# Other PSUM banks for scores, query features and the output product, and other slots for their steps, in a fused graph-transformer kernel

## The reference

```python
# attention of layer i, per head (8 heads of 64, 256 random features)
qp = softmax_kernel(q, proj[i], True)        # exp(q @ proj.T - diag - max over features) + eps
o = einsum('bhmd,bhnm,bhn->bhnd', ctx, qp, d_inv)
x = x + o @ Wo[i] + bo[i]
y = layernorm(x, ln2_g[i], ln2_b[i])
x = x + gelu(y @ W1[i] + b1[i]) @ W2[i] + b2[i]      # 512 -> 2048 -> 512
# product-key memory on the normed sum of the branches
q1, q2 = halves of (x @ Wq + bq).reshape(-1, 8, 128)
s1t, i1 = top_k(q1 @ keys[:, 0].T, 8); s2t, i2 = top_k(q2 @ keys[:, 1].T, 8)   # 256 keys each
scores, best = top_k(all 64 sums of s1t and s2t, 8)  # -> 64 table rows per node
inner = einsum('bd,bhkd->bhk', x, w_down[indices])
out = einsum('bhk,bhkd->bd', relu(inner) * softmax(scores), w_up[indices])
```

## Time and profile before

| | us |
|---|---|
| median of 3 runs | 2603.11 (2601.43 to 2609.05) |
| the profiled execution, its own time | 2612.62 |
| its span in the trace | 2610.8 |
| PE busy / DVE / POOL / ACT over the span | 2223.4 (85%) / 1453.7 (56%) / 1034.6 (40%) / 742.2 (28%) |
| DMA, mean over the span | 204 GB/s |

### The profile page before, as it was taken

How to read it: one execution, slowest core, us unless ns; L and a number is a source line. 1 busy time by engine, 2 the same in 40 slices (tenths; PEclk the granted TensorE clock), 3 DMA queues, 4 the chain that set the end, 5 groups by cost and what they waited for, 6 DMA issues and landing times.

```text
span 2610.8 us, 29611 instructions
## 1 busy us (share of the span) xinstructions
PE 2223.4 (85%) x10300; PEld 1263.6 (48%) x10300; DVE 1453.7 (56%) x3917; ACT 742.2 (28%) x1837; POOL 1034.6 (40%) x886
## 2 busy tenths in 40 slices
PE   3999989999499999999999997888878888788643
PEld 2666656676244444444565674444434444444200
DVE  3765665643466630000133547777877778678775
ACT  1346231121010001100134523434334343343222
POOL 0036877773111100000000005655656566566775
PEclk9999999999699999999999999889989898898755
DMA  9944145557847760043202417989989899899998
GB/s 299 289 113 134 2 82 113 126 117 162 218 138 192 194 152 2 9 131 108 59 1 32 149 45 259 342 306 333 345 308 346 316 325 342 306 332 337 349 385 347
DMA packets 242915, 531.73 MB, mean 204 GB/s; under 512 B 103774, under 2 KB 105173, under 8 KB 238611
## 3 DMA queue, kind: packets, MB, share of 16 engines
q0 software_dynamic: 170032, 379.99, 44.1%
q1 hardware_dynamic: 64413, 144.24, 18.5%
q10 hardware_dynamic: 8330, 5.71, 0.8%
HBM read 493.10 MB, written 48.92 MB: 208 GB/s over the span
## 4 chain that ended last, share of the span: by engine, by line
PE 67%; DVE 19%; DMA 7%; issue 3%; ACT 2%; POOL 2%; SPq 0%; POOLq 0%; DVEq 0%; ACTq 0%
PE bank L1154 13%; PE bank L1131 5%; PE bank L987 4%; PE bank L998 4%; PE bank L1493 4%; PE bank L1476 4%; PE bank L1484 3%; PE bank L1363 3%; PE bank L748 3%; PE bank L650 3%; PE bank L671 3%; PE bank L1141 2%; PE bank L658 2%; DMA stage<-xn_d 2%; PE bank L874 2%
## 5 line engine op out<-in xcount | busy, mean ns | idle before, releaser
L1334 POOL DMA_INDIRECT qv<-in_L_ffn_rows,qv x162 | 160.7, 992 | 754.6 <-DVE qv L1749 645.0
L1639 ACT ACTIVATE stage<-stage,qv 128x32 f32<-128x32 f32 x640 | 204.6, 321 | 471.5 <-DVE ring_more L1859 124.0
L310 POOL DMA_INDIRECT adj<-e_cnt,e_idx x80 | 166.4, 2080 | 211.4 <-issue 186.7
L1476 PEld LDWEIGHTS bank<-stage,big 128*128 128x128 f32 x1280 | 173.5, 202 | 98.6 <-issue 72.0
L1334 POOL DMA_INDIRECT big<-in_L_ffn_rows,qv x160 | 162.6, 1016 | 112.3 <-PE bank L1493 74.2
L1476 PE MATMUL bank<-stage,big 128*128 128x125 f32 x1280 | 184.9, 291 | 23.4 <-ACT stage L1606 22.8
L1334 POOL DMA_INDIRECT ring_more<-in_L_ffn_rows,qv x159 | 160.2, 1008 | 106.6 <-PE bank L1493 70.0
L310 POOL DMA_INDIRECT adj_b<-e_cnt,e_idx x80 | 169.0, 2112 | 52.4 <-issue 27.4
L1334 POOL DMA_INDIRECT h<-in_L_ffn_rows,qv x159 | 160.5, 1009 | 48.5 <-issue 45.1
L1154 PE MATMUL bank<-big,wreg 125*125 125x512 f32 x400 | 172.0, 592 | 0.0
L1154 PE MATMUL bank<-big,qv 125*125 125x512 f32 x400 | 171.8, 592 | 0.0
(11 more groups left out here) (259 smaller groups left out, 4019.7 us busy)
## 6 DMA issues: line engine op xcount, KB each, us to landing
wreg<-in_L_gnn_basis SPq DMA_DIRECT2D x30, 1024.0 KB, 5.6
stage<-in_L_gnn_basis POOLq DMA_DIRECT2D x45, 512.0 KB, 4.9
big<-in_L_mix_W SPq DMA_DIRECT2D x4, 4096.0 KB
adj<-adj_b POOLq DMA_DIRECT2D x9, 1328.1 KB, 25.8
adj<-wreg SPq DMA_DIRECT2D x5, 2187.5 KB
adj_b<-wreg SPq DMA_DIRECT2D x5, 2187.5 KB
wreg<-adj SPq DMA_DIRECT2D x10, 1093.8 KB
qv<-adj SPq DMA_DIRECT2D x10, 1093.8 KB
```

The lines of the kernel that those rows point to most:

```text
L310: nc.gpsimd.indirect_dma_start(out=(adj, adj_b)[g % 2], out_offset=bass.IndirectOffsetOnAxis(ap=e_idx[:, g:g + 1], axis=0), in_=e_cnt[:, g ...
L1334: nc.gpsimd.indirect_dma_start(out=ring[place(t, s)], out_offset=None, in_=a["L0_ffn_rows"], in_offset=bass.IndirectOffsetOnAxis(ap=slots_ ...
L1476: mm = nc.tensor.matmul(psum[F_BANKS[n % 2]][:, 0:P], w1_sb[:, k, 128 * n:128 * n + 128], y1_t[:, k, :], start=(k == 0), stop=(k == KC - 1))
L1639: nc.scalar.activation(wsel[:, s % DRING, :], mask, ACT.Relu, scale=inner[:, s:s + 1]).then_inc(p_diag, 1)
```

## The change

Even heads' scores go to banks 0 and 6, odd heads' to 3 and 4; features u alternate between banks 6 and 3; the output product goes to bank 2. Waits follow the banks. The tables move: the turn of x from step 3 to 4, the second feature from 3 to 2, scores of heads 1 to 7 one step earlier, the best of each head one step later, the attention's layer norm one step earlier, the feed-forward from steps 28 to 59 into 29 to 55, and `finish` from steps 61 to 63 to 57 to 61. The code of the loop stands 4 lines further down.

```diff
-        TURN_AT = 3
-        QUERY_AT = [4 + hh - hh // 2 for hh in range(PKH)]
-        SCORE_AT = [10 + 4 * hh for hh in range(PKH)]
-        SEARCH_AT = SCORE_AT[0] + 1
-        TAIL_AT = SEARCH_AT + 4 * PKH - 1
+        TURN_AT = 4
+        QUERY_AT = [5 + hh // 2 for hh in range(PKH)]
+        SCORE_AT = [10] + [9 + 4 * hh for hh in range(1, PKH)]
+        SEARCH_AT = SCORE_AT[0] + 2
+        TAIL_AT = SEARCH_AT + 4 * PKH - 2
...
-        MLP_AT = 28
-        LATE_PE = [0, 3, 3, 5, 6, 6, 8, 9, 9, 11, 12, 14, 17, 19, 20, 27] + [MLP_AT + n for n in range(2 * HC)]
+        MLP_AT = sorted([29 + n for n in range(2 * HC - 5)] + [31 + 4 * n for n in range(5)])
+        LATE_PE = [0, 2, 3, 5, 6, 6, 8, 9, 9, 11, 12, 14, 17, 19, 20, 27] + MLP_AT
-        LATE_DVE = [2, 5, 8, 10, 11, 16, 22, 22, 23, 24, 25, 25, 26, 26] + [61, 61, 62, 62, 63, 63, 63, 63, 63]
+        LATE_DVE = [2, 5, 8, 10, 11, 16, 21, 21, 22, 23, 24, 24, 25, 25] + [57, 57, 58, 58, 59, 59, 60, 60, 61]
...
+        def score_bank(hh, s):
+            return ((0, 6), (3, 4))[hh % 2][s]
+        def feature_bank(u):
+            return (6, 3)[u % 2]
...
                     pe.wait_ge(p_q, t * PKH + hh + 1)
-                    elif hh:
-                        pe.wait_ge(p_top, t * TOPN + 4 * hh)
-                    elif t:
-                        pe.wait_ge(p_xr, 4 * t)
+                    if hh == 0:
+                        pe.wait_ge(p_keysS, 4)
+                        pe.wait_ge(p_q, t * PKH + QB)
+                    if hh < 2 and 1 <= t <= TILES - PRE:
+                        pe.wait_ge(m["qx"], late_from["qx"] + KC * (t - 1) + 3 + hh)
+                    if hh == 1 and t:
+                        pe.wait_ge(p_xr, 4 * t)
+                    if hh >= 2:
+                        pe.wait_ge(p_top, t * TOPN + 4 * (hh - 1))
...
                 def features(u):
-                    if u:
-                        pe.wait_ge(m["qx"], late_from["qx"] + k4 + u)
-                    elif T > PRE:
-                        pe.wait_ge(m["hat"], late_from["hat"] + 2 * (T - PRE - 1) + 1)
+                    if u == 1:
+                        pe.wait_ge(p_xr, 4 * (T - PRE) + 3)
+                    if u >= 2:
+                        pe.wait_ge(m["qx"], late_from["qx"] + k4 + u - 1)
...
-                    mm = nc.tensor.matmul(psum[6][0:P, :], o1_t[:, P * k:P * k + P], wreg[:, 3, 512 * k:512 * k + 512],
+                    mm = nc.tensor.matmul(psum[2][0:P, :], o1_t[:, P * k:P * k + P], wreg[:, 3, 512 * k:512 * k + 512],
```

More of the change, by code:

```diff
@@ L1288, in pieces @@
             return out
-        LATE_ACT[10:] = [MLP_AT + n + 1 for n, what in enumerate(pieces()) if what[0] == "f1"]
+        LATE_ACT[10:] = [MLP_AT[n] + 1 for n, what in enumerate(pieces()) if what[0] == "f1"]
         def mem_sp(sp):
@@ L1370, in front @@
                     pe.wait_ge(p_q, t * PKH + hh + 1)
[L1371 to L1375, removed]
-                    elif hh:
-                        pe.wait_ge(p_top, t * TOPN + 4 * hh)
-                    elif t:
+                    if hh == 0:
[4 more added lines that the diff above has]
+                    if hh == 1 and t:
                         pe.wait_ge(p_xr, 4 * t)
+                    if hh >= 2:
+                        pe.wait_ge(p_top, t * TOPN + 4 * (hh - 1))
                     for s in range(2):
                         rows = slice(64 * s, 64 * s + 64)
-                        mm = nc.tensor.matmul(psum[score_bank(t, hh) + s][0:P, 0:NKEYS], pq_t[rows, hh, :], keys_t[rows, hh, :], start=True, stop=True)
+                        mm = nc.tensor.matmul(psum[score_bank(hh, s)][0:P, 0:NKEYS], pq_t[rows, hh, :], keys_t[rows, hh, :], start=True, stop=True)
                     mm.then_inc(p_s_pe, 1)
@@ L1390, in features @@
                     pe.wait_ge(s_q, 16 * (TILES - PRE) + 16 * (T - PRE + 1))
-                    if u:
-                        pe.wait_ge(m["qx"], late_from["qx"] + k4 + u)
-                    elif T > PRE:
-                        pe.wait_ge(m["hat"], late_from["hat"] + 2 * (T - PRE - 1) + 1)
-                    nc.tensor.matmul(psum[6][0:P, :], q1_t[:, u, :], projbd[:, :], start=True, stop=True).then_inc(m["qd_pe"], 1)
+                    if u == 1:
+                        pe.wait_ge(p_xr, 4 * (T - PRE) + 3)
+                    if u >= 2:
+                        pe.wait_ge(m["qx"], late_from["qx"] + k4 + u - 1)
+                    nc.tensor.matmul(psum[feature_bank(u)][0:P, :], q1_t[:, u, :], projbd[:, :], start=True, stop=True).then_inc(m["qd_pe"], 1)
                 def turn(u):
@@ L1691, in top @@
                 for s in range(2):
-                    nc.vector.max(top_v[:, hh, s, :], psum[score_bank(t, hh) + s][0:P, 0:NKEYS]).then_inc(p_top, 1)
+                    nc.vector.max(top_v[:, hh, s, :], psum[score_bank(hh, s)][0:P, 0:NKEYS]).then_inc(p_top, 1)
                 n += 2
@@ L1696, in top @@
                     dve.wait_ge(p_top, n)
-                    nc.vector.max_index(top_i[:, hh, s, :], top_v[:, hh, s, :], psum[score_bank(t, hh) + s][0:P, 0:NKEYS]).then_inc(p_top, 1)
+                    nc.vector.max_index(top_i[:, hh, s, :], top_v[:, hh, s, :], psum[score_bank(hh, s)][0:P, 0:NKEYS]).then_inc(p_top, 1)
                     yield
@@ L1806, in attend @@
                     dve.wait_ge(s_h, 16 + 16 * (T - HBUFS + 1))
-                nc.vector.tensor_tensor(h_of(T), psum[6][0:P, :], h_of(T), ALU.add).then_inc(m["hat"], 1)
+                nc.vector.tensor_tensor(h_of(T), psum[2][0:P, :], h_of(T), ALU.add).then_inc(m["hat"], 1)
                 yield
@@ L1891, in mem_dve @@
                         take(t - 1)
-                    if SEARCH_AT <= s < TAIL_AT and (s - SEARCH_AT) % 4 < 3:
+                    if SEARCH_AT <= s < TAIL_AT and (s - SEARCH_AT) % 4 < 2:
+                        next(ahead, None)
+                    if SEARCH_AT <= s < TAIL_AT and (s - SEARCH_AT) % 4 == 1:
                         next(ahead, None)
```

6 lines of the change are left out of this document (2 added, 4 removed).

## The result

The changed kernel took **2571.46 us** (median of 3 runs, 2568.45 to 2573.01) against 2603.11 before: a ratio of 0.9885, 95% interval 0.9862 to 0.9907, 31.6 us faster. The forecast was 2561, so its direction was right and the time lies within its range; a quarter of the gain that it promised did not come. The profiled execution took 2573.01 (span 2571.2), 1.6 over its median; that of before was 9.5 over its own.

The account below looks back on a forecast made before the run. No single engine bounds it throughout; engines wait for each other along a 105.5 us chain. Stage terms +4.4 - 3.3 + 0.6 - 6.9 = -5.2 per heavy tile, 41.6 over eight, gave 2561 us, range 2536 to 2591.

Parts of the forecast that it names:

- A: Stage from last f2 to first query: 4.4 us longer per tile, 20.1; bounds 1.6 to 6.4 more.
- the clock charge: Between last f2 and first query, PE idles and transposes and rows run at 1.2 GHz: 1.7 us more.
- the charge of 1.1 for the gathers: After the last f2, the next tile's row 0 lands at 10.9, DVE wants it at 9.8: 1.1 us more.
- B: Stage from first query to output product: 3.3 us less per tile, between 1 and 3.8 less.
- C: Stage from output product to first f1: 0.6 us more per tile, from 0 to 1.5.
- D: Stage from first f1 to last f2: 6.9 us less per tile, so 40.2.
- that tail is late because DVE stood 5.21 us at the scores of head 5: Between first f1 and last f2: scores moved ahead of f1 remove this DVE wait and PE's 1.64 us idle.
- The 1.64: PE's idle us between first f1 and last f2, where the search's tail is late; claimed to go.
- No charges: Rival: after the last f2 clock stays up, gathers land in time; 8.0 us per tile, 2536; chance 0.15.
- No change: Rival: DVE's dots behind the last f2 cost over four times 0.67, cancelling the gain: 2603; chance 0.09.
- Gathers starve: Rival: between first f1 and last f2, rows outpace DMA; 103 us per tile, 2.5 less, 2583; chance 0.17.
- The slower rival: The same starving with transfers at the heavy tile's 362 GB/s: 8.3 us more per tile, 2669; chance 0.09.

Follow-up runs that it names:

- ring of 13: The changed kernel with 13 ring buffers instead of 12, and three node buffers h instead of four: 2555.12 us, ratio 0.9822.
- the banks alone: The changed kernel (new banks and start order) with feed-forward and `finish` back in their old places: 2592.23 us, ratio 0.9955 against the kernel before.
- the earlier copy: The changed kernel with ACT's copy of the turned attention output behind dot 17 instead of dot 18: 2559.75 us, ratio 0.9841.
- the feed-forward alone: The kernel before with only the feed-forward and `finish` tables of the change, banks and start as before: 2603.32 us, ratio 1.0001.

## Why the prediction was right, and where it was wrong

*The whole.* Seven periods are shorter by 3.45 on the mean instead of 5.2; times eight that is 27.6 (the eighth heavy tile, the first, lies outside these periods; it takes 3.1 less from its first gather to its output, much like the others). The two light tiles gave 2.4 (allowed: up to 3). That makes 30.0 of the 31.6 between the medians. The rest of the 39.6 between the two spans lies before the loop: its first f1 starts 9.8 earlier in the profile of after, in code that is the same.

*A, right in kind, mis-sized.* Forecast +4.4, measured +6.4. From the norm's end to the first query it is 7.4, the forecast to a tenth, with the transposes (1.09, 0.83) and rows (1.87) at the 1.2 GHz level that the clock charge assumed (granted clock 0.50 from 1784.63 to 1788.42). **The step that failed is the charge of 1.1 for the gathers.** Without late landings the norm ends at 12.3 (ring of 13), against 11.6 in the sum; with them at 14.5. So the charge is 2.2, and DVE's own way 0.7 longer than counted. The trace of after shows what I left out. The buffers of rows 0 to 3 are free by 1.97 after the last f2 (1.9 in the prediction), and issue and landing take 9.46 (0.94 + 8.1). But I let POOL issue row 0 as soon as its buffer is free. POOL is still at rows 62 and 63 then and comes to row 0 3.6 after the last f2 in the tile read above, 2.6 to 3.6 in all seven. And I charged row 0, while the norm stands behind dot 1: its gather is issued one place later, at 3.9 to 4.9, and dot 1 stands idle for it for 1.3 to 1.7 in every tile. A came out at the upper bound (6.4), but not by the longer latency that the bound was made of.

*B, right.* -3.2 against -3.3; the banks alone give -3.0. That close a match is luck, for two errors lie in it and cancel: the gross gain is larger (with the earlier copy B is 4.9 shorter), and PE now waits 2.4 for the copy before the product with Wo (0.7 before). I had put the delay at the rows of step 16, and at 0.5.

*C, direction right, outside its bounds.* +1.9 against +0.6 (0 to 1.5). Three of seven tiles have 17.8, which is +0.9; four have 19.5, those whose product with Wo ran in part at the lower clock level behind that new wait. The 1.7 between them is the product itself (5.4 and 3.7), a term that the sum does not have. What decides the level there stays open. Taking the wait away did not shorten C, since more dots then stand in its way (the run with the earlier copy).

*D, nearly right, for partly wrong reasons.* -8.5 against -6.9. **The step that failed is "that tail is late because DVE stood 5.21 us at the scores of head 5"**: with the banks alone DVE waits 3.5 less at heads 5 to 7 and the tail is no earlier; with the feed-forward alone it waits nearly as before and PE's wait is gone. The 1.64 did go, but not shown by that route: PE comes to the spread later, and in the change the tail is also earlier. The rest is what left the stage, and the clock. For one tile before and one after, in the windows of D, and the f1 in the same windows by line (busy, mean ns):

```profile
1846.50:1893.63 47.13, 45.38 (x308) 25.92 (x312) 35.37 (x125) 20.30 (x55) 30.93 (x31) 0.95 0.89 332
```

```profile
1829.54:1868.69 39.15, 38.66 (x281) 23.77 (x282) 32.05 (x114) 16.05 (x47) 27.91 (x27) 0.98 0.92 330
```

```profile
L1476 PE MATMUL bank<-stage,big 128*128 128x125 f32 x128 | 18.9, 294 | 2.6 <-ACT stage L1606 2.6
```

```profile
L1480 PE MATMUL bank<-stage,big 128*128 128x125 f32 x128 | 17.8, 287 | 0.5 <-ACT stage L1615 0.5
```

PE's idle time falls from 1.75 to 0.49, its busy time by 6.7. Of this the work that the prediction took out is 5.3. The same 128 f1 matmuls give 1.1, which I did not count: the rows and scores ahead of them now take the 1.2 GHz level that followed the wait (the granted clock of the stage rose from 0.95 to 0.98). The gelu, which I took as 0, costs 0.5 in this tile and nothing in the other six.

*The rivals.* "No charges" fell: both charges came. "No change" named the right place: DVE's way to the norm costs more than four dots, by 2.9 of the 5 that it asked for. "Gathers starve" put the starving into D and gave 103 per tile (its terms, 85 + 9.4 + 8, add up to 102.4): its time of 2583 is 12 off, and the ring shows its mechanism at work, in A. The slower rival needed landings "some 3 us over the 8.1 of rows 9"; in A they are 1.2 over it (9.3, last section), though with one buffer less the whole gain is gone.

## What to carry to other kernels

When work is moved ahead of a point where a consumer catches up with a ring of buffers, count for the very row that it needs: when its buffer comes free, how many issues stand ahead of it in the queue, and the landing. A stage that gets shorter can pay less than it should if the ring was sized for the old one; try one buffer fewer and one more in both kernels before moving pieces again. And a wait of 2 us on TensorE may charge its neighbour through the clock; taking it away pays only as far as nothing else has become just as late.

## What was not expected of the hardware

**With half the bytes the light tiles are no shorter.** I left them as they were because their DMA share is near its limit. With half the bytes they took 85.8 and 89.8 us all the same, after 88.0 and 83.9 with whole rows. The stretch of a light tile with half gathers, and POOL's timeline in it:

```profile
2380.00:2460.00 80.00, 36.07 (x212) 8.04 (x210) 62.22 (x206) 22.12 (x64) 62.94 (x57) 0.64 0.67 189
```

```profile
2409.44 1.16 POOL L1338 DMA_INDIRECT h<-in_L_ffn_rows,qv  x1 [0.30 <-issue]
2410.90 1.16 POOL L1338 DMA_INDIRECT h<-in_L_ffn_rows,qv  x1 [0.30 <-issue]
```

The DMA is busy 0.67 of the time and moves 189 GB/s, while POOL issues one gather behind the other, 80 us / 57 = 1.40 us each. Issue there does not get cheaper with the bytes, and 64 times 1.40 is 89.8. So with half the bytes these tiles are bound by POOL's issue. The Trainium skill, page "Perfetto Trace Analysis", section "What 'DMA-bound' means", has this case: a kernel can be bound by the engine that issues, whose track is then solid DMA work; this trace agrees, with its 62.94 of 80 us busy and 0.30 between two issues.

With whole rows POOL issues nearly without a stop too, in the last tile of after 1.28 us apart (63 steps in 80.8 of its 83.9 us). The 409 GB/s from which the prediction took its 85 us of transfers are such a stretch as well: 38 gathers in 48 us, 1.26 each, at a DMA share of 1.03. Which of the two binds whole rows is not shown, nor why issue is slower beside half the bytes.

**A landing is much longer than its transfer.** In stage A of after POOL's gathers show this time to landing:

```profile
DMA to landing us min/median/max: 7.5/9.3/10.7
```

The last tile of before has a median of 8.1. A gather of 512 KB takes 1.3 us at 409 GB/s, so several are always under way. DVE, when it catches up, takes a row every 0.67 us: it can use up what has landed before the next gathers land, and the ring of 13 shows that one buffer more is then enough.
